# Two-layer cross-attention kernel: the fifth slot's unit order, with the output projection first

## The chip, the cores and the metric

The kernel runs on one core of a Trainium2 chip. The metric is the device time of one execution in microseconds. All matrix work is float32, part of it with operands rounded to a shorter form and a second, low part beside them.

## The reference

Sixteen batch entries go through two cross-attention layers, one after the other.

```python
# layer 0, 8 heads of 40
hs     = mha(x @ Wq, enc @ Wk, enc @ Wv)            # 112 queries, 371 keys
ca_hs1 = mha(ca_q1, x, x)                           # queries from the 4 token rows
ca_hs2 = mha(ca_hs1 @ Wq, ca @ Wk_ca, ca @ Wv_ca)   # 4 keys
x1     = (hs + ca_hs2) @ Wout + b_out + x
# layer 1, 20 heads of 16
out    = mha(x1 @ Wq, ctx @ Wk, ctx @ Wv) @ Wo + bo + x1   # 375 keys
```

`x` is 16 x 112 x 320, `ctx_768` is 16 x 375 x 192; the last 4 of its 375 rows are `ca`, the others `enc`.

## The kernel before

The program is a software pipeline written out by hand. An iteration t (18 of them, `ITERATIONS`) has seven slots. Each slot scores one group of four heads: slots 0 and 1 the two groups of layer 0 of batch entry t, slots 2 to 6 the five groups of layer 1 of entry t-1. A group's work is spread over three slots:

- In its own slot TensorE computes the scores in two pairs of heads into `bankS` (L1156 for layer 0, L1159 for layer 1), and VectorE takes the negated maxima of each pair (`maximum`, L773). The second pair has to wait until the first pair's maximum is taken, as both use `bankS`.
- One slot later the maxima are transposed on TensorE (`transpose_m`, L1172), copied by VectorE (`copy_mT`, L779) and put into a row of the query tile by a transfer that ScalarE's queue issues (`place_m`, L588).
- Two slots later (`LAG`) the shifted, transposed scores are computed (`shifted_scores`, L1187 and L1193), ScalarE takes the exponentials (`exps`, L573 to L577), and TensorE multiplies with the values (`attend`, L1225) into `bankO`, which VectorE copies out (`copy_o`, L790).

Between these, each slot has four phases with *units*, the projections and transposes of the layers. A unit fills one of two PSUM banks, `bankX[0]` and `bankX[1]`, on TensorE, and ScalarE or VectorE or both drain it. The banks are handed out by place in the list of all units (`ORDER`), alternately: a unit may start when the unit two places earlier has been drained.

```python
def bank(name, b):
    return AT[name, b] % 2
def drained(name, b):
    return AT[name, b] // 2 + 1
```

The table `UNITS` says for each slot which units stand in its four phases, with the batch entry's offset from t. All engines walk the same table in the same order, each in its own strict queue. On TensorE a slot runs: scores of pair 0; phase 0; the shifted scores of the group two slots back; the maxima's transpose of the group one slot back; phase 1; scores of pair 1; phase 2; the attention product; phase 3. On VectorE the maximum of pair 0 comes first, then phase 0, the maxima's copy, in the fifth slot `reciprocal2` (L877), phase 1, the maximum of pair 1, phase 2, `copy_o`, phase 3. On ScalarE: phase 0, the exponentials, the maxima's placement, then phases 1, 2 and 3.

The units that matter here, all in or next to the fifth slot (i = 4):

- `K0_0`, `K0_1`, `K0_2`: the keys of layer 0 for entry t+1, in three parts of five matmuls (L1005). ScalarE rounds the bank into a high part (L625), VectorE subtracts it from the bank for the low part (L814), which frees the bank. SyncE then spreads the keys by transfers (L342 to L347).
- `p3T` (L1098): the four tokens' shares, one transpose. It waits for VectorE's split of `p3`; ScalarE copies it out (L684).
- `N0` (L1095): layer 0's attention output, four transposes of `o0T`. VectorE drains it: reciprocals of the sums (L795) and the division into `hn0` (L797).
- `out1` (L1005, operands `act_hi`, `act_lo`): the output projection of layer 1 for entry t-2, eight accumulating matmuls. Its input is `hn1T`, drained in the fourth slot. VectorE adds the residual (L872), which frees the bank.
- `q0T_0` (L1071): four transposes of the next entry's queries, drained by ScalarE (L658).
- `hn0T` (L1087): three transposes of `hn0` in the sixth slot, drained by ScalarE (L680, L681) and VectorE (L863, L866). `V0_0` (L1005) follows it.
- GpSimd's `normalise2` (L464) multiplies the second attention's probabilities by their reciprocal sums, about when the fifth slot ends.

`out1` exists for t from 2 to 17, `p3T` and `N0` for t up to 15, the K0 units for t up to 14, and layer 1's groups for t from 1 to 16.

Of the kernel before, what the change touches and what calls it, by code (L numbers as in the profile page):

```python
# [47 lines left out]
    ([("q1T_1", -1), ("V1_2", -1)], [("q1T_2", -1)], [("q0", 1)], [("N1a", -2), ("K1_0", 0)]),  # L48
    ([("K1_1", 0)], [("S3", 0), ("S2_0", 1)], [("N1b", -2)], [("S2_1", 1)]),
    ([("K1_2", 0)], [("K0_0", 1)], [("hn1T", -2)], [("K0_1", 1)]),  # L50
    ([("K0_2", 1)], [("p3T", 0), ("N0", 0)], [("out1", -2)], [("q0T_0", 1)]),
    ([("hn0T", 0), ("V0_0", 1)], [("q0T_1", 1)], [("out0", 0)], [("T2_0", 1)]),
    ([("x1T", 0), ("V0_1", 1)], [("T2_1", 1)], [("q1", 0)], [("V0_2", 1)]),
]
# [1289 lines left out]
```

## Time and profile before

| | |
|---|---|
| median of three runs | 756.53 us (755.18 to 759.52) |
| the profiled execution, its own time | 753.38 us |
| its span, first to last instruction | 751.5 us |
| TensorE matmuls busy | 703.0 us, 94% |
| TensorE weight loads busy | 610.3 us, 81% |
| VectorE busy | 472.3 us, 63% |
| ScalarE busy | 404.0 us, 54% |
| GpSimd busy | 295.5 us, 39% |
| mean granted TensorE clock | 0.983 of full speed |

Shares are of the span. Matmuls are pipelined and their ends modelled, so records of consecutive matmuls overlap, and the distance between two starts tells more than the length of a record. In the rows of the trace PE is TensorE's matmul, PEld its weight load, DVE is VectorE, ACT ScalarE, POOL GpSimd and SP SyncE; a trailing q is an engine's queue. A bracket at a row's end gives the idle time of the engine before it and what ended that. The chain of waits follows the work that ended last back from the last instruction, at each step to what released it. L12 is line 12 of the kernel.

### The profile page before, as it was taken

Reading aid. Unit: us, or ns where it says so; the run is one execution under the profiler, and the core shown is the slowest. Engines: PE = TensorE matmul, PEld = TensorE weight load, DVE = VectorE, ACT = ScalarE, POOL = GpSimd, SP = SyncE. Lnnn points to the kernel's source line nnn. Section 1 sums busy time; section 2 is a strip of 40 time slices with the busy share of each in tenths; the row PEclk is TensorE's granted clock in tenths of the full one; section 3 lists DMA queues with packets and bytes.
Section 4 is the critical chain, followed back from the end, with each engine's and each line's share of the span. In section 5 each row is a group of like instructions: output and inputs, shape, how many; then the busy total and the mean of one; then the engine's idle time right before and its main releaser. Section 6 shows DMA issues by size and latency. Waiting matters only on the chain.

```text
span 751.5 us, 18194 instructions
## 1 busy us (share of the span) xinstructions
PE 703.0 (94%) x6924; PEld 610.3 (81%) x6924; DVE 472.3 (63%) x1028; ACT 404.0 (54%) x923; POOL 295.5 (39%) x401
## 2 busy tenths in 40 slices
PE   8787999999999999999999999999999999999975
PEld 5586888888888888888888888888888888888763
DVE  2653666657576665757576575756667575766662
ACT  2454555555565555565555555556555555654432
POOL 5485662444334253433325344323524542330300
PEclk9889999999999999999999999999999999999996
DMA  9533553443516244252524434261533425051400
GB/s 325 175 96 96 112 133 75 107 80 79 133 47 143 62 119 95 67 118 54 137 60 125 92 80 103 62 142 45 136 81 94 89 76 129 20 137 28 87 7 11
DMA packets 52387, 72.45 MB, mean 96 GB/s; under 512 B 12128, under 2 KB 44256, under 8 KB 52304
## 3 DMA queue, kind: packets, MB, share of 16 engines
q1 hardware_dynamic: 44832, 60.34, 31.7%
q0 software_dynamic: 6144, 9.25, 6.5%
q10 hardware_dynamic: 1328, 1.71, 0.6%
q8 instruction: 57, 0.93, 0.5%
q14 instruction: 26, 0.21, 0.1%
HBM read 20.60 MB, written 4.26 MB: 33 GB/s over the span
## 4 chain that ended last, share of the span: by engine, by line
PE 69%; ACT 13%; DVE 8%; issue 3%; POOL 1%; DMA 1%; SPq 1%; ACTq 0%; POOLq 0%
PE bankX L1005 28%; PE bankO L1225 8%; PE bankST L1193 7%; ACT arena L577 7%; PE bankS L1159 6%; PE bankST L1187 5%; ACT arena L595 3%; DVE negmax L773 2%; DVE q1T L829 2%; PE bankX L1118 2%; PE bankX L1125 2%; PE bankX L1087 2%; PE bankS L1156 2%; ACT q1T L666 2%; PE bankX L1071 2%
## 5 line engine op out<-in xcount | busy, mean ns | idle before, releaser
L773 DVE TENSOR_REDUCE negmax<-bankS 112x2 f32<-112x750 f32 (+1 forms) x224 | 208.7, 932 | 57.0 <-PE bankS L1159 32.7
L494 POOL DMA_DIRECT2D k_stack<-stage x192 | 96.6, 511 | 181.5 <-DVE stage L809 153.9
L577 ACT ACTIVATE arena<-bankST 125x1344 f32<-125x1344 f32 x80 | 103.5, 1294 | 30.9 <-PE bankST L1193 30.9
L1225 PE MATMUL bankO<-arena,v 125*32 125x112 f32 (+2 forms) x2688 | 107.2, 264 | 6.2 <-ACT arena L577 4.4
L1225 PEld LDWEIGHTS bankO<-arena,v 125*32 125x32 f32 (+2 forms) x2688 | 81.2, 117 | 29.0 <-issue 12.7
L1159 PE MATMUL bankS<-k_stack,q1T 112*112 112x376 f32 x320 | 87.8, 355 | 4.1 <-DVE negmax L773 3.0
L1005 PE MATMUL bankX<-ctx_hi,WH 128*120 128x376 f32 (+2 forms) x192 | 69.0, 360 | 3.0 <-DVE qn L765 2.2
L457 POOL TENSOR_TENSOR w2bd<-w2s,cst 96x896 fp32r<-96x896 f32 x16 | 29.9, 1870 | 98.4 <-DVE w2s L765 98.4
L1005 PE MATMUL bankX<-WH,ctx_hi 128*125 128x320 f32 x192 | 66.1, 344 | 0.1
L1193 PE MATMUL bankST<-q1T,k_stack 112*125 112x224 f32 x480 | 65.4, 272 | 0.0
L1005 PE MATMUL bankX<-ctx_hi,WL 128*120 128x376 f32 (+2 forms) x192 | 64.0, 334 | 0.0
L1193 PEld LDWEIGHTS bankST<-q1T,k_stack 112*125 112x125 f32 x480 | 62.0, 188 | 0.8 <-DMA q1T<-mT 0.4
L1005 PE MATMUL bankX<-WL,ctx_hi 128*125 128x320 f32 x192 | 58.5, 312 | 0.0
L1159 PEld LDWEIGHTS bankS<-k_stack,q1T 112*112 112x112 f32 x320 | 49.4, 177 | 8.8 <-DVE negmax L773 6.5
L829 DVE TENSOR_SCALAR q1T<-bankX,odd_rows 128x448 fp32r<-128x448 f32 (+1 forms) x48 | 29.1, 606 | 41.7 <-ACT q1T L666 41.2
L595 ACT ACTIVATE arena<-bankX,negmax 112x112 f32<-112x112 f32 x128 | 43.6, 354 | 21.7 <-DVE negmax L837 21.6
L1005 PE MATMUL bankX<-WH,act_hi 128*112 128x320 f32 x144 | 46.7, 325 | 3.3 <-DVE act_hi L866 1.4
L483 POOL TENSOR_TENSOR xb<-xp,bias_sb 112x320 f32<-112x320 f32 x16 | 13.9, 867 | 88.7 <-DVE x L860 88.6
L779 DVE CAST mT<-bankO 4x112 fp32r<-4x112 f32 x112 | 29.0, 259 | 30.0 <-PE bankO L1172 30.0
L1187 PEld LDWEIGHTS bankST<-q0T,k_stack 121*125 121x125 f32 (+1 forms) x384 | 46.0, 187 | 0.0
L619 ACT ACTIVATE stage<-bankX 128x376 fp32r<-128x376 f32 (+1 forms) x48 | 23.1, 482 | 41.7 <-PE bankX L1005 41.0
L1187 PE MATMUL bankST<-q0T,k_stack 121*125 121x112 f32 (+1 forms) x384 | 44.9, 266 | 0.0
(141 smaller groups left out, 1545.8 us busy)
## 6 DMA issues: line engine op xcount, KB each, us to landing
k_stack<-stage SPq DMA_DIRECT2D x96, 176.2 KB
k_stack<-stage SPq DMA_DIRECT2D x192, 70.5 KB, 2.6
k_stack<-stage POOLq DMA_DIRECT2D x192, 47.0 KB, 2.0
ctx_raw<-in_ctxT SPq DMA_DIRECT2D x16, 376.0 KB, 3.3
k_stack<-stage SPq DMA_DIRECT2D x48, 117.5 KB
xp<-in_xpad SPq DMA_DIRECT2D x16, 224.0 KB, 3.3
x_raw<-in_xT SPq DMA_DIRECT2D x16, 168.0 KB, 2.4
out<-x1b SPq DMA_DIRECT2D x16, 140.0 KB, 3.2
```

The costliest lines, as they stand in the source:

```text
L457: nc.gpsimd.tensor_tensor(w2bd[:, :, :], w2s[:, :].bitcast(F32).unsqueeze(1).broadcast_to((96, H0, SQ)), mask96.unsqueeze(2).broadcast_to( ...
L494: pool.dma_start(dst, src).then_inc(k1_stacked_pool[b % 2], 16)
L577: nc.scalar.activation(dst[0:KC], bankST[0:KC, :, 0:GROUP * SQ], ACT.Exp).then_inc(exp_done, 1)
L595: last = nc.scalar.activation(prob2[0:SQ, h, :], X[0:SQ, (h % 4) * SQ:(h % 4 + 1) * SQ], ACT.Exp, bias=negmax2[:, h:h + 1], accum_out=sum2 ...
L773: nc.vector.tensor_reduce(negmax[:, n % 2, 2 * pair:2 * pair + 2], bankS[0:SQ, :, 0:keys], axis=AX, op=ALU.max, negate=True).then_inc(max_ ...
L779: nc.vector.tensor_copy(mT[:, n % MT_BUFS, :], bank_mT).then_inc(mT_copied, 1)
L829: nc.vector.tensor_scalar(q1T[:, 4 * i:4 * i + g, 1, :], X[:, 0:g * SQ].rearrange("p (h q) -> p h q", h=g), odd_rows[:, :], None, ALU.mult ...
L1005: last = nc.tensor.matmul(dst, lhs, rhs, start=(n == 0), stop=(n == len(passes) - 1))
L1159: last = nc.tensor.matmul(bankS[0:SQ, j, 0:SKP], q1T[0:ROWS1, h // 2, h % 2, :], k1_stack[b % 2][0:ROWS1, h // 2, :], start=True, stop=True)
L1187: last = nc.tensor.matmul(bankST[0:keys, c, SQ * j:SQ * j + SQ], k0_stack[0:M_ROW0 + 1, h, KC * c:KC * c + keys], q0T[0:M_ROW0 + 1, h, :], ...
L1193: last = nc.tensor.matmul(bankST[0:KC, c, 2 * SQ * pair:2 * SQ * pair + 2 * SQ], k1_stack[b % 2][0:ROWS1, 2 * k + pair, KC * c:KC * c + KC ...
L1225: last = nc.tensor.matmul(dst, v, src[0:keys, c, SQ * j:SQ * j + SQ], start=(c == 0), stop=(c == NKC - 1))
```

## The change

One row of the table is written differently: in the fifth slot `out1` goes from phase 2 to phase 1, and `p3T` and `N0` from phase 1 to phase 2.

```diff
-    ([("K0_2", 1)], [("p3T", 0), ("N0", 0)], [("out1", -2)], [("q0T_0", 1)]),
+    ([("K0_2", 1)], [("out1", -2)], [("p3T", 0), ("N0", 0)], [("q0T_0", 1)]),
```

On TensorE, from the maxima's transpose (L1172) to the attention product (L1225) of the fifth slot of iteration 2, the piece of the difference up to the part that both have in common (the removed rows behind it are the same scores and `out1`, further down):

```order
 L1172 MATMUL bankO<-cst,negmax 4x112 [waits o_copied,mT_copied,max_done]
-L1098 MATMUL bankX<-cst,p3w 96x112 [waits p3_split,bank_drained1]
-L1095 MATMUL bankX<-cst,o0T 112x128 [waits o_copied,bank_drained0]
+L1005 MATMUL bankX<-WH,act_hi 112x320 [waits bank_drained0,bank_drained1]
+L1005 MATMUL bankX<-WL,act_hi 112x320
+L1005 MATMUL bankX<-WH,act_lo 112x320
...
+L1159 MATMUL bankS<-k_stack,q1T 112x376 [waits max_done]
+L1159 MATMUL bankS<-k_stack,q1T 112x376
+L1098 MATMUL bankX<-cst,p3w 96x112 [waits p3_split,bank_drained0]
+L1095 MATMUL bankX<-cst,o0T 112x128 [waits o_copied,bank_drained1]
 L1095 MATMUL bankX<-cst,o0T 112x128 x3
```

The eight matmuls of `out1` now come first, then the scores of pair 1, then `p3T` and `N0`. `p3T` and `N0` swap banks with each other, and `out1`, which used the bank that `p3T` had left, now uses the one that `K0_1` left; `N0` gets it after `out1`.

On VectorE, the same slot:

```order
 L779 CAST mT<-bankO 4x112 [waits mT_done]
 L877 RECIPROCAL rsum<-sum 112x8 [waits bank_drained1]
-L795 RECIPROCAL r<-bankX 112x8 [waits unit_filled]
-L797 TENSOR_TENSOR hn<-bankX,r 112x320 [waits rec_done]
-L773 TENSOR_REDUCE negmax<-bankS 112x2 [waits scores_done]
-L872 TENSOR_TENSOR x1b<-bankX,x1b 112x320 [waits x1b_ready,unit_filled]
+L872 TENSOR_TENSOR x1b<-bankX,x1b 112x320 [waits x1b_ready,unit_filled]
+L773 TENSOR_REDUCE negmax<-bankS 112x2 [waits scores_done]
+L795 RECIPROCAL r<-bankX 112x8 [waits unit_filled]
+L797 TENSOR_TENSOR hn<-bankX,r 112x320 [waits rec_done]
 L790 COPY o1T<-bankO 128x112 [waits pv_done]
```

The drain of `out1` goes ahead of the maximum of pair 1, and the two steps that drain `N0` go behind it. The queues of ScalarE, GpSimd and SyncE read the same before and after.

## Rows read from the trace of the kernel before

**Rows 1.** The page, busy time of each engine with its share of the span.

```profile
PE 703.0 (94%) x6924; PEld 610.3 (81%) x6924; DVE 472.3 (63%) x1028; ACT 404.0 (54%) x923; POOL 295.5 (39%) x401
```

**Rows 2.** The page, the chain that ended last, by engine.

```profile
PE 69%; ACT 13%; DVE 8%; issue 3%; POOL 1%; DMA 1%; SPq 1%; ACTq 0%; POOLq 0%
```

**Rows 3.** The chain in order of time, fifth slot of t=6: start us, us, what.

```profile
313.30 1.29 ACT arena L577
314.59 0.10 ACTq L588
...
314.74 0.27 ACT p3T L684
...
315.05 1.42 PE bankX L1005 x8
...
317.72 0.34 PE bankS L1159 x2
```

**Rows 4.** Timeline, same slot: start us, us, engine, line, operation, count, idle before.

```profile
313.10 0.26 PE L1172 MATMUL bankO<-cst,negmax 112*4 112x112 f32 x1
313.20 0.26 PE L1098 MATMUL bankX<-cst,p3w 112*96 112x112 f32 x1
...
313.37 0.54 DVE L814 TENSOR_TENSOR stage<-bankX,stage 80x376 fp32r<-80x376 f32 x1
...
313.96 0.65 PE L1095 MATMUL bankX<-cst,o0T 128*112 128x128 f32 x4 [0.50 <-DVE stage L814]
...
314.36 0.59 PE L1159 MATMUL bankS<-k_stack,q1T 112*112 112x376 f32 x2
314.64 0.21 DVE L795 RECIPROCAL r<-bankX 112x8 f32<-112x8 f32 x1 [0.46 <-PE bankX L1095]
...
314.89 0.49 DVE L797 TENSOR_TENSOR hn<-bankX,r 112x320 f32<-112x320 f32 x1
...
315.29 0.31 PE L1005 MATMUL bankX<-WL,act_hi 128*112 128x320 f32 x1
...
315.30 0.93 DVE L773 TENSOR_REDUCE negmax<-bankS 112x2 f32<-112x750 f32 x1
...
315.54 1.68 POOL L464 TENSOR_TENSOR arena<-arena,rsum 112x896 f32<-112x896 f32 x1
...
316.17 0.31 PE L1005 MATMUL bankX<-WL,act_hi 128*112 128x320 f32 x1
...
316.40 0.78 PE L1225 MATMUL bankO<-arena,v 125*32 125x112 f32 x24
316.51 0.49 DVE L872 TENSOR_TENSOR x1b<-bankX,x1b 112x320 f32<-112x320 f32 x1 [0.28 <-PE bankX L1005]
```

**Rows 5.** What TensorE waited for at tile o0T, and at line 1005: us, times.

```profile
  DVE stage L814: 18.2, 30
...
  ACT p3T L684: 6.9, 15
```

**Rows 6.** Timeline of TensorE: N0 in t=1 and 14; scores, out1 in t=15.

```profile
98.77 0.65 PE L1095 MATMUL bankX<-cst,o0T 128*112 128x128 f32 x4 [0.50 <-DVE stage L814]
...
660.50 0.65 PE L1095 MATMUL bankX<-cst,o0T 128*112 128x128 f32 x4 [0.51 <-DVE stage L814]
...
699.35 0.59 PE L1159 MATMUL bankS<-k_stack,q1T 112*112 112x376 f32 x2
...
700.49 0.40 PE L1005 MATMUL bankX<-WH,act_hi 128*112 128x320 f32 x1 [0.55 <-ACT p3T L684]
```

**Rows 7.** Timeline of VectorE, t=6: the subtraction that frees K0_1's bank.

```profile
311.95 0.55 DVE L814 TENSOR_TENSOR stage<-bankX,stage 120x376 fp32r<-120x376 f32 x1
```

**Rows 8.** Timeline of TensorE, t=6: q0T_0 and hn0T behind the attention product.

```profile
317.12 0.60 PE L1071 MATMUL bankX<-cst,qn 112*120 112x112 f32 x4
...
317.90 0.45 PE L1087 MATMUL bankX<-cst,hn 112*128 112x112 f32 x3
```

**Rows 9.** What the DMA queue of SyncE waited for: us, times, longest us.

```profile
SPq L342 <- DVE stage L814: 235.9, 15, 21.5
```

## The prediction

> **What bounds the kernel now.** I read the page's busy shares first. TensorE is busy for 94% of the span, no other engine above 63% [rows 1]. The chain of waits says the same with a reservation: 69% of it is TensorE, 13% ScalarE and 8% VectorE [rows 2]. So most of the time TensorE's own work sets the pace, and what a reordering can win is the time in which it stands still. The change touches one slot in seven, so I then followed the chain through one such slot, iteration t=6, at 313 to 317 us of the span. There it does not run through TensorE at all: for 1.75 us it is the exponentials of the group before, a short mask copy's issue, ScalarE's copy of p3T, and only then the first pass of out1 [rows 3]. The reader should see that out1 waits for the PSUM bank in which p3T lies, and p3T's drain of 0.26 us stands in ScalarE's queue behind exponentials of 1.29 us.
>
> The timeline of the same slot shows a second stall [rows 4]. p3T's transpose starts at 313.20. A transpose that is ready starts 0.10 us after the instruction before it (313.10 to 313.20), so N0's could start at 313.30; it starts at 313.96, just after VectorE has subtracted K0_2's low part (313.37 + 0.54 = 313.91) out of the bank N0 is to use. **Stall one: 0.66 us.** The scores of pair 1 start at 314.36 and hold TensorE for 0.35 (0.34 in the chain at 317.72, where nothing waits [rows 3]), so out1 could start at 314.71; it starts at 315.05. **Stall two: 0.34 us.**
>
> Both repeat: the wait of the N0-type transposes for that subtraction is 18.2 us in 30 records, and the wait of the output projections for p3T's copy is 6.9 us in 15 [rows 5]. Records of idle time are shorter than my stalls, since a matmul's modelled end lies after the start of the next; I count start to start. N0 waits so in each of the fourteen iterations t=1 to 14, of which the first and the last are shown; t=15 has no K0 units, hence only stall two, there longer [rows 6].
>
> **The change part by part.** No instruction is added, removed or resized. Banks are handed out alternately in the order of units, so three units change place and bank; ScalarE's, GpSimd's and SyncE's queues keep their order word for word, and no transfer is moved past another.
>
> 1. out1 comes right after the maxima's transpose. It takes the bank of K0_1, whose subtraction ended at 311.95 + 0.55 = 312.50 [rows 7], and p3T's old start, 313.20. Its eight passes: the first 0.24 (315.05 to 315.29), then seven of 0.147 (315.29 to 316.17 in six steps), 1.27 in all [rows 3, 4]. The scores of pair 1 start at 314.47; the maximum they wait for stands before K0_2's subtraction in VectorE's queue, which began at 313.37, so they find it done.
> 2. p3T takes K0_2's bank, free since 313.91, and starts at 314.47 + 0.35 = 314.82. Stall one is gone: out1 and the scores cover it. Without that cover it would cost its 0.66 again.
> 3. N0 takes out1's bank, and this is the new wait. Now VectorE's drain of out1 (L872) starts 0.34 after the start of the last pass (316.17 to 316.51) and takes 0.49 [rows 4]. The last pass would start at 314.32, so the drain runs 314.66 to 315.15; VectorE is free then: it sat idle for 0.46 before 314.64. N0 follows 0.05 later, as it did behind the subtraction: 315.20. It could have begun at 314.92. **New stall: 0.28 us.** Nothing in the trace has this wait, so I bound it: zero if the drain were hidden, 0.66 if it were as long as the wait it replaces. I take the 0.28 built from out1's own rows.
> 4. N0 takes 0.40 (313.96 to 314.36), the step to the attention product 0.08 more than a plain step (0.23 less 0.147), so that starts at 315.68 instead of 316.40. Its exponentials ended at 314.59. It holds TensorE 0.72 and q0T_0 starts at 316.40, against 317.12 [rows 4, 8].
>
> Gain per iteration: 0.66 + 0.34 - 0.28 = **0.72 us**.
>
> The Trainium skill has a rule on this, in "Perfetto Trace Analysis", section Optimizing Tensor Performance: independent matmul groups should rotate through different PSUM banks, so that one group's evacuation overlaps the next one's matmuls. The new order obeys it, and by the rule alone the new stall would be nil and the gain 1.00. The rows speak against the full overlap: what stands between out1 and N0 is 0.35 + 0.10 us of TensorE work, the evacuation 0.88 from the last pass's start to N0's.
>
> What is late next: N0's division. It moves behind the maximum of pair 1 on VectorE. That maximum starts when its scores and the drain before it are done, at 315.12 or so (now 315.30), and ends 0.93 later, at 316.05; reciprocal and division take 0.25 and 0.49 from start to start and end (314.64, 314.89, 315.38 now), less 0.08 of overlap, so hn is ready at 316.71. hn0T would want it at 316.40 + 0.78 = 317.18 (317.12 to 317.90 now) [rows 8]. Margin 0.47, cost nothing. The copy of the attention's output behind it is short, and the next maximum needs scores that start only after q0T_0. p3T's copy on ScalarE ends near 315.4, q0T_0 needs that bank at 316.40: free. Out of the slot everything moves up together: V0_0 follows q0T_0's copy as before. SyncE waits 235.9 us in all, 15 times, for K0_2's subtraction [rows 9], so its queue has room in an iteration shorter by 0.7.
>
> **Sum.** t=2 to 14: 13 x 0.72 = 9.4. t=1 has no out1; the scores move ahead of p3T and N0, so they cover 0.35 of stall one at least, and all 0.66 at most if they find their bank free; the maximum also no longer stands behind N0's division: I take 0.6. t=15 loses stall two, 700.49 less 699.70 = 0.79, and gets the new stall of 0.28: 0.5 [rows 6]. t=0 has neither scores nor out1, so nothing changes. In t=16 out1 alone is left of the three and goes ahead of the second scores instead of behind them, which moves work within one slot: 0. Together 10.5 us. The profiled execution took 753.4, so it would take 742.9. The median of the three runs lies 3.15 above that execution, and I forecast for the median: 756.5 - 10.5 = **746.0 us**, 1.4% less.
>
> **Rivals.**
>
> *The division falls into GpSimd's window.* GpSimd's normalisation (L464) runs 315.54 to 317.22; the division, today outside it, would run 316.22 to 316.71, inside. If it were held until 317.22, hn would be ready at 317.71 and hn0T 0.58 late: gain 0.14 per iteration, 13 x 0.14 + 1.1 = 2.9, so 753.6 us. Against it: out1's drain runs inside that window now, 316.51, at 0.49 [rows 4]. Chance 4%. The Trainium skill, "SBUF — State Buffer", says VectorE and GpSimd share a port pair held as an exclusive lock, against VectorE instructions in a two-port mode or with two SBUF inputs; the division reads one operand from PSUM, so even by the rule it should pass.
>
> *Taken back elsewhere.* A later wait that is hidden now (the division, a copy on ScalarE, a mask's transfer) grows by most of 0.72. For it: 21% of the chain is ScalarE and VectorE. Against: those steps start from TensorE's own results and move with them. If half is taken back, 751 us; if all, 756.5. Chance 10%, 4% of it for all.
>
> *Slower: out1 itself waits.* All later work of the slot now stands behind out1, so any delay of its start is paid by scores, N0 and the attention product. The place is its bank and its operands: K0_1's drain and hn1T's split. It decides from 0.72 us on. Had out1 to wait behind a copy queued after exponentials as p3T's is (1.75 us), each iteration would be 1.03 longer and the time 756.5 + 13 x 1.03 = 770. Against: its bank is free 0.7 us before it is wanted [rows 7]. Chance 4%.
>
> **How the numbers follow.** Forecast 82%, port window 4%, taken back 10%, slower 4%. The forecast's own range comes from the bounds: stalls all gone, 13 x 1.00 + 1.6 = 14.6 gives 741.9; a new stall of 0.66, 13 x 0.34 + 1.1 = 5.5 gives 751.0. The runs shown lie up to 3 us from their median, so I set 741 to 752, which leaves out about 15%. Half a percent, 3.8 us, is about what a measurement of this kernel tells from no change. Faster by more: the 82% and most of the half-way cases, 0.88. Within: 0.08. Slower: 0.04.
>
> **What would show it.** Right: N0's idle time before it is put down to L872 and not L814, with starts 0.38 after p3T's; no wait for p3T's copy (L684) in t=2 to 14; from the maxima's transpose to q0T_0 3.3 us instead of 4.0; the iteration 42.6 instead of 43.3 us ((660.50 - 313.96) / 8); busy times as before. Wrong: hn0T waiting for L797, a gap before out1, N0 later than 315.9 on this slot's clock, or a span within 4 us of 751.5.

## The result, and the profile after

The changed kernel took 744.82 us (median of 4 runs, 743.47 to 745.48), the kernel before 755.86 us beside it: the ratio is 0.984, with a 95% interval of 0.981 to 0.988. In two later comparisons the changed kernel came to 0.985 [0.980, 0.990] and 0.986 [0.984, 0.987]. The forecast was 746.0 us, range 741 to 752.

The page of the kernel after has nearly the same busy times as before, to 0.8 us on TensorE's matmuls and 2.3 us on its weight loads; the chain lost a part of ScalarE's share [rows 1, 2]. First its busy times, then the chain by engine:

```profile
PE 702.2 (94%) x6924; PEld 612.6 (82%) x6924; DVE 470.8 (63%) x1028; ACT 403.7 (54%) x923; POOL 294.8 (40%) x401
...
PE 73%; ACT 10%; DVE 9%; issue 3%; POOL 1%; ACTq 0%; POOLq 0%
```

The chain of waits through the fifth slot of t=6, to be held against [rows 3] (start us, us, what):

```profile
309.49 0.10 PE bankO L1172
309.59 1.19 PE bankX L1005 x8
310.77 0.02 issue
310.80 0.50 DVE x1b L872
311.30 0.04 issue
311.35 0.65 PE bankX L1095 x4
311.99 0.71 PE bankO L1225 x24
```

Neither the exponentials nor p3T's copy stand in it any more. In their place is out1's own drain, L872, with N0 (L1095) behind it. The timeline of the same slot, against [rows 4, 8]:

```profile
309.33 0.26 PE L1172 MATMUL bankO<-cst,negmax 112*4 112x112 f32 x1
309.36 0.38 PE L1005 MATMUL bankX<-WH,act_hi 128*112 128x320 f32 x1
...
310.45 0.31 PE L1005 MATMUL bankX<-WL,act_hi 128*112 128x320 f32 x1
310.60 0.51 PE L1159 MATMUL bankS<-k_stack,q1T 112*112 112x376 f32 x2
310.80 0.49 DVE L872 TENSOR_TENSOR x1b<-bankX,x1b 112x320 f32<-112x320 f32 x1 [0.38 <-PE bankX L1005]
310.95 0.26 PE L1098 MATMUL bankX<-cst,p3w 112*96 112x112 f32 x1
...
311.35 0.65 PE L1095 MATMUL bankX<-cst,o0T 128*112 128x128 f32 x4
311.76 1.68 POOL L464 TENSOR_TENSOR arena<-arena,rsum 112x896 f32<-112x896 f32 x1
311.92 0.78 PE L1225 MATMUL bankO<-arena,v 125*32 125x112 f32 x24
...
312.28 0.49 DVE L797 TENSOR_TENSOR hn<-bankX,r 112x320 f32<-112x320 f32 x1
312.64 0.60 PE L1071 MATMUL bankX<-cst,qn 112*120 112x112 f32 x4
...
313.42 0.45 PE L1087 MATMUL bankX<-cst,hn 112*128 112x112 f32 x3
```

From the maxima's transpose (L1172) to q0T_0 (L1071) it is 312.64 - 309.33 = 3.31 us; before it was 317.12 - 313.10 = 4.02. That is 0.71 less, against 0.72 forecast. N0 starts 0.40 after p3T, of which 0.10 is the plain step, so the new stall is 0.30 (0.28 forecast).

What TensorE waited for at the transposes of L1095 is, in place of the first row of [rows 5]:

```profile
  DVE x1b L872: 6.2, 14
```

Outside the slot, PV2 (L1125), the unit that multiplies the second attention's probabilities with their values once per iteration, gives a ruler: the start of its first matmul. Its second and last starts are at 77.17 and 680.10 us before, and at 77.22 and 669.91 after:

```profile
77.22 0.99 PE L1125 MATMUL bankX<-arena,xp 112*64 112x112 f32 x16
...
669.91 0.99 PE L1125 MATMUL bankX<-arena,xp 112*64 112x112 f32 x16 [0.26 <-DVE q1T L829]
```

Between them lie the fifth slots of t=1 to 14. This middle stretch went from 602.93 to 592.69 us, 10.2 less, and the iteration (the median step of the twelve from t=2 on) from 43.32 to 42.60.

### The profile page after: what moved, and what is told of

Its sections match the earlier page's. It is cut to its first block, busy times and chain, and to the rows that moved or that the text cites. A ratio compares the mean times of both kernels' runs of the same rounds, so it can differ in the third digit from the quotient of the medians.

```text
span 743.6 us, 18194 instructions
## 1 busy us (share of the span) xinstructions
PE 702.2 (94%) x6924; PEld 612.6 (82%) x6924; DVE 470.8 (63%) x1028; ACT 403.7 (54%) x923; POOL 294.8 (40%) x401
## 4 chain that ended last, share of the span: by engine, by line
PE 73%; ACT 10%; DVE 9%; issue 3%; POOL 1%; ACTq 0%; POOLq 0%
PE bankX L1005 29%; PE bankO L1225 8%; PE bankST L1193 7%; PE bankS L1159 6%; PE bankST L1187 5%; ACT arena L577 4%; ACT arena L595 3%; DVE q1T L829 2%; DVE negmax L773 2%; PE bankX L1118 2%; PE bankX L1125 2%; PE bankX L1087 2%; PE bankS L1156 2%; PE bankX L1071 2%; ACT q1T L666 2%
## 5 line engine op out<-in xcount | busy, mean ns | idle before, releaser
L1225 PE MATMUL bankO<-arena,v 125*32 125x112 f32 (+2 forms) x2688 | 107.8, 265 | 6.1 <-ACT arena L577 4.6
L1225 PEld LDWEIGHTS bankO<-arena,v 125*32 125x32 f32 (+2 forms) x2688 | 81.6, 118 | 28.6 <-issue 13.6
L1005 PE MATMUL bankX<-WL,act_hi 128*112 128x320 f32 x144 | 45.1, 313 | 0.0
```

What stands on the lines that cost most here:

```text
L1005: last = nc.tensor.matmul(dst, lhs, rhs, start=(n == 0), stop=(n == len(passes) - 1))
L1225: last = nc.tensor.matmul(dst, v, src[0:keys, c, SQ * j:SQ * j + SQ], start=(c == 0), stop=(c == NKC - 1))
```

## The experiments

The table has all runs. *Middle* is the stretch just named, *tail* runs from the last PV2 to TensorE's last record; both, like the iteration, are read from one profiled execution. The ratio is to the kernel before on the same chip.

| kernel | iteration | middle | tail | median us | ratio [95%] |
|---|---|---|---|---|---|
| before | 43.32 | 602.93 | 68.44 | 755.9 | |
| the change | 42.60 | 592.69 | 70.72 | 744.8 | 0.984 [0.981, 0.988] |
| e1_scores_first | 43.31 | 602.33 | 67.97 | 755.1 | 0.999 [0.995, 1.002] |
| e2_p3T_vector | 42.99 | 598.44 | 71.18 | 752.4 | 0.997 [0.994, 0.999] |
| e3_no_scores_between | 43.09 | 599.69 | 69.13 | 751.3 | 0.997 [0.993, 1.000] |
| e4_tail_as_before | 42.61 | 593.40 | 69.85 | 747.0 | 0.988 [0.982, 0.993] |
| e5_N0_after_attend | 42.40 | 591.37 | 71.01 | 742.7 | 0.982 [0.978, 0.987] |
| e6_V0_before_hn0T | 42.49 | 592.44 | 69.14 | 743.9 | 0.985 [0.980, 0.989] |
| e7_longer_drain | 43.00 | 598.71 | 72.05 | 753.3 | 0.997 [0.993, 1.001] |
| after_again | 42.61 | 592.98 | 68.09 | 743.9 | 0.985 [0.980, 0.990] |
| e5_again | 42.38 | 591.36 | 70.22 | 741.9 | 0.983 [0.981, 0.985] |
| after_third | 42.59 | 593.40 | 69.14 | 744.0 | 0.986 [0.984, 0.987] |

**e1: cover stall one alone.** The scores of pair 1 go ahead of p3T, N0 and out1; out1 stays last of the three.

```diff
-    ([("K0_2", 1)], [("p3T", 0), ("N0", 0)], [("out1", -2)], [("q0T_0", 1)]),
+    ([("K0_2", 1)], [], [("p3T", 0), ("N0", 0), ("out1", -2)], [("q0T_0", 1)]),
```

> The kernel before, with p3T, N0 and out1 all in phase 2, in their old order and banks: the scores of pair 1 move ahead of them. Theory (the slot is bound by the exponentials followed by p3T's copy on ScalarE, on which out1 waits; stall one lies inside that wait): N0 still starts at 313.96 on the old clock or a little later, out1 still at 315.05, the iteration stays 43.3 us and the time 755.9, within 0.3%. Rival (stall one is worth its 0.66 us by itself, and covering it alone brings it in): 14 x 0.66 = 9 us less, 747, iteration 42.7.

Its timeline in the fifth slot:

```profile
317.46 0.26 PE L1172 MATMUL bankO<-cst,negmax 112*4 112x112 f32 x1
...
317.86 0.27 PEld L1159 LDWEIGHTS bankS<-k_stack,q1T 112*112 112x112 f32 x2 [0.40 <-DVE negmax L773]
317.86 0.60 PE L1159 MATMUL bankS<-k_stack,q1T 112*112 112x376 f32 x2
...
318.30 0.26 PE L1098 MATMUL bankX<-cst,p3w 112*96 112x112 f32 x1
...
318.39 0.60 PE L1095 MATMUL bankX<-cst,o0T 128*112 128x128 f32 x4
...
319.40 0.40 PE L1005 MATMUL bankX<-WH,act_hi 128*112 128x320 f32 x1 [0.41 <-ACT p3T L684]
```

N0 now follows p3T without a stall (0.09), and nothing is won: out1 starts 1.94 after the maxima's transpose, where it was 1.95 before. The iteration is 43.31. Most of the 0.66 us turned up in two other places. The scores of pair 1 now start 0.40 behind the transpose, of which a plain step is 0.10 at most; their weight load waited for the first pair's maximum (317.86). And the stall in front of out1 grew from 0.34 to 0.61 (from N0's start and its 0.40, 318.79, to 319.40), since p3T's copy ends no earlier in ScalarE's queue. The theory holds, the rival of 9 us falls. So the two stalls of the prediction are not independent: the first lies in the shadow of the second.

**e2: take p3T's copy out from behind the exponentials.** The order stays that of before; ScalarE skips the unit and VectorE does the copy.

```diff
-                if kind in ("out0", "out1", "N0", "N1a", "N1b"):
+                if kind in ("out0", "out1", "N0", "N1a", "N1b", "p3T"):
...
-                elif kind == "p3T":
-                    nc.scalar.activation(p3T[:, :], X[0:96, 0:SQ], ACT.Copy).then_inc(free, 1)
...
+                elif kind == "p3T":
+                    dve.wait_ge(unit_filled, filled(name, b))
+                    nc.vector.tensor_copy(p3T[:, :], X[0:96, 0:SQ]).then_inc(free, 1)
```

> The kernel before, with p3T's copy on VectorE and no longer behind the exponentials on ScalarE. Theory: stall two goes (0.34 us in t=2 to 14, 0.79 in t=15), stall one stays: 13 x 0.34 + 0.8 = 5.2 us less, iteration 42.98, time 750.7, idle time before N0 still put down to L814. Rival (what out1 waits for is in truth something else, or the wait moves to the maxima on VectorE): iteration 43.3, time 755.9.

In its timeline the lines of TensorE stand one higher by number:

```profile
354.50 0.26 PE L1173 MATMUL bankO<-cst,negmax 112*4 112x112 f32 x1
...
355.36 0.65 PE L1096 MATMUL bankX<-cst,o0T 128*112 128x128 f32 x4 [0.51 <-DVE stage L812]
355.52 0.21 DVE L849 CAST p3T<-bankX 96x112 fp32r<-96x112 f32 x1
355.77 0.59 PE L1160 MATMUL bankS<-k_stack,q1T 112*112 112x376 f32 x2
356.20 0.31 PE L1006 MATMUL bankX<-WH,act_hi 128*112 128x320 f32 x1
```

out1 starts 0.43 after the scores with no idle time, N0 still waits for the subtraction. From the maxima's transpose (354.50) to q0T_0, which starts at 358.18, it is 3.68 us, 0.34 less than the 4.02 of before. The iteration is 42.99, 0.33 less, as the theory has it (42.98). The middle is 4.5 us shorter; of the 5.2 us expected in the time, the ratio shows 2.6, with an interval up to 4.8. The price of stall two is confirmed per iteration, that of the whole time only in part.

**e3: the change without the scores between out1 and N0.**

```diff
-    ([("K0_2", 1)], [("out1", -2)], [("p3T", 0), ("N0", 0)], [("q0T_0", 1)]),
+    ([("K0_2", 1)], [("out1", -2), ("p3T", 0), ("N0", 0)], [], [("q0T_0", 1)]),
```

> The changed kernel, with p3T and N0 in phase 1 directly behind out1 and ahead of the scores of pair 1. On VectorE N0's division then goes ahead of the maximum of pair 1. Theory: N0 starts 0.05 after out1's drain as in the change, so its stall grows by the scores' 0.35 to 0.64; and the maximum, behind the division, ends about 1.4 us later than in the change, so that the next slot's scores wait for it about 0.4. Together the gain of the change is gone: iteration 43.2 to 43.4, time 754 to 756. Rival (only the cover of N0 counts, VectorE's order does not): 0.35 per iteration less gain, iteration 42.95, time 749.7.

```profile
356.58 0.26 PE L1098 MATMUL bankX<-cst,p3w 112*96 112x112 f32 x1
...
357.32 0.65 PE L1095 MATMUL bankX<-cst,o0T 128*112 128x128 f32 x4 [0.49 <-DVE x1b L872]
...
358.66 0.93 DVE L773 TENSOR_REDUCE negmax<-bankS 112x2 f32<-112x750 f32 x1
...
359.64 0.27 PEld L1159 LDWEIGHTS bankS<-k_stack,q1T 112*112 112x112 f32 x2 [0.30 <-DVE negmax L773]
```

N0 starts 0.74 after p3T, a stall of 0.64 as expected, and the next slot's scores wait 0.30 for the maximum (0.4 expected), a wait that the change does not have. But the iteration is 43.09, 0.2 below before, where the theory had 43.2 to 43.4 and the rival 42.95; the time of 751.3 us also lies between the theory's 754 to 756 and the rival's 749.7. Both named stalls are there, so VectorE's order does count. The theory's sum was too high because it left out that V0_0, which follows, waits for q0T_0's copy on ScalarE in the other two kernels (its weight loads for 3.1 us in 13 records before, 3.4 in 14 in the change, none in e3), and that this wait takes up a part: from q0T_0 to V0_0 it is 1.34 us in e3 and 1.23 in the change, so of the 0.30 only 0.11 is paid. The scores between out1 and N0, with VectorE's order that comes with them, are worth 43.09 - 42.60 = 0.49 us per iteration.

**e7: lengthen out1's drain** in the changed kernel by a copy whose result nobody reads.

```diff
+                    nc.vector.tensor_copy(hn1[:, :], X[0:SQ, 0:HID])
                     nc.vector.tensor_tensor(y[:, :], X[0:SQ, 0:HID], y[:, :], ALU.add).then_inc(free, 1)
```

> The changed kernel with out1's drain lengthened: VectorE first copies the bank, 112x320, into a buffer that is not read any more, then does the addition. Theory (N0 waits for out1's drain, and what it waits is paid in full): the copy adds about 0.4 us to the drain, N0 starts that much later, iteration 43.0, time 744.8 + 14 x 0.4 = 750.4. Rival (the drain is hidden in part, the chain through the scores and maxima sets the pace): iteration under 42.75, time under 747.

```profile
357.02 0.49 DVE L872 COPY hn<-bankX 112x320 f32<-112x320 f32 x1 [0.37 <-PE bankX L1006]
357.17 0.26 PE L1099 MATMUL bankX<-cst,p3w 112*96 112x112 f32 x1
357.43 0.48 DVE L873 TENSOR_TENSOR x1b<-bankX,x1b 112x320 f32<-112x320 f32 x1
...
357.96 0.65 PE L1096 MATMUL bankX<-cst,o0T 128*112 128x128 f32 x4 [0.54 <-DVE x1b L873]
```

The addition starts 0.41 later and N0 0.79 instead of 0.40 after p3T. The iteration is 43.00: 0.40 more, all of it paid. (The median of 753.3 us lies above the 750.4 expected; the middle grew by 6.0 us, and this profile has the longest tail of all.) So the new stall is real, is out1's drain, and has no slack behind it.

**e5: hide the new stall.** N0 goes behind the attention product, which covers the drain.

```diff
-    ([("K0_2", 1)], [("out1", -2)], [("p3T", 0), ("N0", 0)], [("q0T_0", 1)]),
+    ([("K0_2", 1)], [("out1", -2)], [("p3T", 0)], [("N0", 0), ("q0T_0", 1)]),
```

> The changed kernel, with N0 behind the attention product instead of ahead of it. Theory: the product of 0.72 us covers out1's drain, so the new stall of 0.3 goes; N0's division then ends about 4.07 us after the maxima's transpose (3.44 in the change), hn0T starts where it did, and V0_0 right behind it 0.15 to 0.2 us earlier than in the change: iteration 42.4, time 742.3 against 744.8. Rival (the later division makes hn0T, and all behind it, late by more than the stall was): iteration 42.85 or more, time 748.

```profile
311.83 0.78 PE L1225 MATMUL bankO<-arena,v 125*32 125x112 f32 x24
...
312.54 0.65 PE L1095 MATMUL bankX<-cst,o0T 128*112 128x128 f32 x4
...
313.47 0.49 DVE L797 TENSOR_TENSOR hn<-bankX,r 112x320 f32<-112x320 f32 x1
...
314.11 0.48 PE L1087 MATMUL bankX<-cst,hn 112*128 112x112 f32 x3 [0.19 <-DVE hn L797]
314.36 0.39 PE L1005 MATMUL bankX<-WH,ctx_hi 128*125 128x320 f32 x1
```

The attention product follows p3T at once, and N0 follows it with no wait. hn0T now does wait for the division, 0.19, which is the wait that the prediction looked for and found to have a margin in the change. The iteration is 42.40 (42.4 expected), the time 742.7.

**e5 again, beside the change**, on one chip:

> The version with N0 behind the attention product once more, timed on the same chip as the changed kernel beside it. From the lengths of the iteration (42.38 against 42.61) theory gives 14 x 0.23 = 3.2 us less than the changed kernel. Rival: the difference is given back at the ends of the program, and the two medians lie within 1 us.

It took 741.88 us, the change 743.99: ratios to before of 0.983 [0.981, 0.985] and 0.986 [0.984, 0.987]. The difference is 2.1 us, between the 3.2 of the theory and the 1 of the rival; the intervals overlap slightly, so the lead rests on the iteration, 42.38 against 42.59, more than on the times. A part is given back right at the start: the step from the second to the third PV2 is 41.0 us in it and 40.5 in the change beside it. The trace of e5_again shows where, in the fifth slot of t=1:

```profile
99.69 0.78 PE L1225 MATMUL bankO<-arena,v 125*32 125x112 f32 x24 [0.44 <-ACT arena L577]
```

There is no out1 in t=1, so the attention product, now directly behind p3T, comes before its exponentials are done and waits for them. From that slot's maxima's transpose to the next one it takes 5.55 us in both executions of e5 and 4.99 in all three of the change. With these 0.56 us taken off, and the iterations of this comparison, the theory's sum is 13 x 0.21 - 0.56 = 2.2 us over the middle, which came out 2.04 shorter (591.36 against 593.40). It is the fastest version found here.

**e6: in e5, V0_0 ahead of hn0T as well.**

```diff
-    ([("hn0T", 0), ("V0_0", 1)], [("q0T_1", 1)], [("out0", 0)], [("T2_0", 1)]),
+    ([("V0_0", 1), ("hn0T", 0)], [("q0T_1", 1)], [("out0", 0)], [("T2_0", 1)]),
```

> As the run before (N0 behind the attention product), and in the sixth slot V0_0 ahead of hn0T, so that they swap banks and V0_0 waits for N0's division and hn0T for q0T_0's copy. Theory: V0_0 starts about 4.1 us after the maxima's transpose, hn0T behind it without a wait, the shifted scores 0.28 us earlier than in the change: iteration 42.3, time 740.9. Rival (hn0T's later drains hold up out0 or q0T_1 in the sixth slot): iteration 42.6 or more, time 744.8 or more.

```profile
315.44 0.45 PE L1087 MATMUL bankX<-cst,hn 112*128 112x112 f32 x3
...
316.90 0.27 DVE L866 TENSOR_TENSOR act_hi<-bankX,act_hi 64x112 fp32r<-64x112 f32 x1
317.20 0.26 DVE L779 CAST mT<-bankO 4x112 fp32r<-4x112 f32 x1
317.24 0.17 PEld L1005 LDWEIGHTS bankX<-WH,act_hi 128*112 128x112 f32 x1 [0.19 <-DVE act_hi L866]
```

42.49: better than the change, but worse than e5, not the 42.3 expected; the time is 743.9 us, 740.9 expected. hn0T starts 0.76 us later relative to the maxima's transpose than in e5 (4.83 against 4.07), its last drain ends at 317.17, and out0 waits for that. The rival named the right place and overstated its price.

**e4, after_again, after_third: the tail.** The profiled execution of the change was 10.2 us ahead at the last PV2 and 7.9 at the end. In e4 the old order is kept for the end of the program:

```diff
+    if t >= 16 and i == 4:
+        phase = {1: 2, 2: 1}.get(phase, phase)
```

> The changed kernel, with the old order of the fifth slot in t=16 and 17 alone. Theory (in t=16 nothing is won or lost by out1's place, and the low clock of the profiled execution's tail is chance): time as the changed kernel's, 744.8, within 0.2%; from the last PV2 (L1125) of the trace to the end 71.0 to 73.5 us, depending on where the clock falls. Rival (out1 ahead of the scores in t=16 costs 0.7 us or brings the early fall of the clock): 0.7 to 2.7 us less, 742 to 744.

> The changed kernel once more, for the length of its iteration and its tail in another execution, beside the two above. Theory: iteration 42.60, time 744.8; the tail from the last PV2 (L1125) to the end is 71 to 73.7 us, with the place where the clock falls differing between executions. Rival (the early fall of the clock at the tail belongs to the change): the tail is 73.5 us again.

> The changed kernel beside the version above. Theory: iteration 42.60, 10.5 to 11 us below the kernel before; the tail behind the last PV2 (L1125) again of another length than in one of the two executions seen (70.72 and 68.09 us), as the clock falls at another place. Rival: the tail is a property of the program and has one of these two lengths to 0.1.

The changed kernel's tail was 70.72, 68.09 and 69.14 us in three executions, e4's 69.85, and over all profiles here it lies between 68.0 and 72.1. (The expectations of e4 and after_again count to the last instruction of the span: that was 73.7 us in the change, 72.8 in e4 and 71.1 in after_again.) The rival of after_third, one of two fixed lengths, falls with 69.14. The tail comes with the granted clock: its mean from the last PV2 to the end is 0.94 in e1 and 0.92 in after_again, which have the shortest tails, 0.88 in the change and 0.84 in e7, which has the longest. Three microseconds from the 45th after the last PV2 on, in the profiles of before, of the change, of after_again and of e1 (the last numbers are the granted clock, the DMA share and GB/s):

```profile
725.10:728.10 3.00, 2.60 (x38) 1.90 (x37) 2.44 (x6) 1.76 (x3) 0.00 (x0) 1.00 0.03 6
```

```profile
714.90:717.90 3.00, 2.72 (x30) 1.98 (x29) 1.94 (x5) 1.74 (x3) 0.00 (x0) 0.52 0.00 1
```

```profile
715.30:718.30 3.00, 2.99 (x30) 2.45 (x33) 2.00 (x4) 1.79 (x3) 0.00 (x0) 0.50 0.00 1
```

```profile
729.40:732.40 3.00, 3.00 (x30) 2.40 (x33) 2.05 (x4) 1.79 (x3) 0.00 (x0) 0.50 0.02 6
```

The clock is at the lower of its two levels for half of that stretch or more in eleven of the twelve profiles (1.2 GHz, 0.50 in the row), e1 with the old tail among them; the profile of before is the one exception. So the early fall does not belong to the change. e4 showed no gain: its median of 747.0 us, of runs from 743.8 to 750.1, is 0.3% above the change's and so outside the 0.2% expected, but its iteration and middle are the change's (42.61 and 593.40). Its profiled execution began 5 us late, with the second PV2 at 82.02. Whether out1's place in t=16 costs a few tenths is below what these runs resolve.

## Why the prediction was right, point by point

- *The two stalls and their causes.* Right in size and cause: e2 took away the second alone and won 0.33 of 0.34, and the change, which covers both, won their sum less the new stall. But the prediction added them as if each could be won alone. e1 shows that the first is worth nothing while the second stands, and that out1's start is fixed by ScalarE's queue. The sum held because the change removes both.
- *Step 1, out1 takes p3T's start.* It started 0.03 after the maxima's transpose, not 0.10, so the scores came 1.27 behind that transpose instead of 1.37. Step 4 was short by as much: from N0's start to the attention product it took 0.57, not 0.48. That the two errors cancel in the 0.71 is luck.
- *Step 3, the new stall.* 0.30 against 0.28. The drain starts 0.35 after the last pass and takes 0.49, as built from the rows of before. e7 shows that it is paid in full. On the Trainium skill's rule on rotating banks ("Perfetto Trace Analysis", Optimizing Tensor Performance), the measurement decides as the rows of before did: rotation alone did not hide the evacuation, and e3 and e5 show that the amount of work placed between is what counts: with 0.10 us between, a stall of 0.64; with 0.45, 0.30; with the attention product as well, none.
- *What is late next: the division.* It ended at 312.28 + 0.49 = 312.77, 0.65 before hn0T started at 313.42; forecast was a margin of 0.47. No cost, as said. It became a wait only in e5.
- *The rival of GpSimd's window.* The division ran inside the normalisation (311.76 to 313.44) at 0.49 us, its old length. No wait. The Trainium skill's rule on the shared port pair ("SBUF — State Buffer", Who interferes with whom) agrees: it asks for a two-port mode or two SBUF inputs, and the division has one input in PSUM.
- *The rival that later waits take it back.* The slot won 0.71 us and the iteration 0.72, so nothing was taken back; V0_0's wait for q0T_0's copy stayed as it was (1.23 us from q0T_0's start in both).
- *The slower rival.* It did not occur: out1 waited for nothing. In e1, where it does wait behind ScalarE's queue, the whole gain is absent.
- *The sum.* For t=2 to 14 it held, 13 x 0.72 = 9.4. For t=1 the prediction took 0.6, and the slot gave 0.3: from its maxima's transpose to the next one it took 5.30 us before and 4.99 in all three executions of the change. The prediction had said "if they find their bank free" of the scores of pair 1 there, and they did not: with no out1 ahead of them they start 0.39 behind the transpose (97.39 to 97.78), as in e1. t=15 won 0.43 instead of 0.5. So the change itself accounts for 9.4 + 0.3 + 0.4 = 10.1 us, against 10.5 forecast. That the middle and t=15 together show 10.2 + 0.4 = 10.7 is luck of these two executions: earlier in t=1, a score matmul waited 0.64 us for a transfer of the keys before, and not at all after (the last section has the rows). The medians differ by 11.0 us, in the later comparisons by 11.2 and 10.8; what makes up the rest over 10.1 is not shown. The forecast of 746.0 also started from a median of 756.5; from the 755.9 measured beside the change it would have been 745.4.

## What to carry to other kernels

When two stalls follow each other in one queue, find out which of them fixes the time at which both end: covering the earlier one may only lengthen the later. A drain of a buffer costs from the last pass's start to the next user's start (here 0.90 us, from 310.45 to 311.35). The last pass itself fills 0.15 of that; the other 0.75 is how much independent work has to stand between the two users. This account gives both stalls measured here: 0.75 less the 0.45 of scores and p3T is 0.30, less the 0.10 of p3T alone 0.65 (0.64 in e3). Count that work before the order is changed, in every iteration: where a unit is missing, as out1 in t=1, so is its cover. And when program ends are noisy, compare the length of a repeated iteration in the traces: here it repeated within 0.02 us for one kernel, while medians of the same kernel moved by 1 us.

## What was not expected of the hardware

The ends of the program vary more than the effect of most single edits. The second PV2 started between 77.16 and 77.96 us in ten of the twelve profiles, and at 82.02 and 82.10 in e4 and e1; from 12 to 22 us of the span these two show a mean granted clock of 0.52, before and the change 1.00. The tail took 68.0 to 72.1 us, with the granted clock falling to its lower level about 45 us after the last PV2 in eleven of the twelve, and again later, at different places. The middle of some 600 us agreed within 0.7 us among three profiles of the changed kernel (592.69 to 593.40), and in e1 within 0.6 us of the kernel before (602.33 and 602.93). Much of what is left of difference there arises in one place, the scores in t=1 that wait for a transfer of keys. Before, and in after_third:

```profile
83.94 0.58 PE L1159 MATMUL bankS<-k_stack,q1T 112*112 112x376 f32 x2 [0.64 <-DMA k_stack<-stage]
```

```profile
84.21 0.56 PE L1159 MATMUL bankS<-k_stack,q1T 112*112 112x376 f32 x2 [0.93 <-DMA k_stack<-stage]
```

The same scores waited 0.36 us in after_again and not at all in the change's first profile, and the middles of the three lie in the same order: 592.69, 592.98 and 593.40.
